# The first expert pass scatters with add into rows that hold x, instead of writing result rows that are summed later

## The reference

```python
def _L0_ffn_ref(x, Wg, W11, W12, W2):
    gate_scores = jax.nn.softmax(x @ Wg, axis=-1)          # E = 8 experts
    topk_scores, topk_idx = jax.lax.top_k(gate_scores, 2)
    topk_scores = topk_scores / (topk_scores.sum(-1, keepdims=True) + 1e-08)
    gate = jnp.einsum('bsh,ehi->bsei', x, W11)             # 256 -> 512
    value = jnp.einsum('bsh,ehi->bsei', x, W12)
    fused = gate * jax.nn.sigmoid(gate) * value
    expert_out = jnp.einsum('bsei,eih->bseh', fused, W2)   # 512 -> 256
    gathered = jnp.take_along_axis(expert_out, topk_idx[..., None], axis=2)
    return jnp.sum(topk_scores[..., None] * gathered, axis=2)

x = x + 0.5 * _L0_ffn_ref(_layernorm(x), Wg, W11, W12, W2)
x = x + _L0_attn_ref(_layernorm(x), ...)   # RMS norm, projections, short convolution, two scans, gate
x = x + 0.5 * _L0_ffn_ref(_layernorm(x), Wg, W11, W12, W2)
```

## Time and profile before

| | us |
|---|---|
| median of three runs | 966.76 |
| lowest and highest | 966.45, 969.17 |
| profiled execution, its own time | 961.58 |
| its span, first to last instruction | 959.8 |

### The profile page before, as it was taken

How to read it: one execution, slowest core, us unless ns; L and a number is a source line. 1 busy time by engine, 2 the same in 40 slices (tenths; PEclk the granted TensorE clock), 3 DMA queues, 4 the chain that set the end, 5 groups by cost and what they waited for, 6 DMA issues and landing times.

```text
span 959.8 us, 19122 instructions
## 1 busy us (share of the span) xinstructions
PE 898.3 (94%) x5429; PEld 773.5 (81%) x5430; DVE 583.2 (61%) x1386; ACT 391.8 (41%) x768; POOL 575.4 (60%) x616
## 2 busy tenths in 40 slices
PE   7869999999999999968999986999999999999994
PEld 7748888888888888846876874788888888888883
DVE  4886565665666655568745987555555555555551
ACT  3834344343443433316635775333333333333331
POOL 4836566655666665427605663577777777777762
PEclk9979999999999999979999987999999999999997
DMA  9743625526345182168202646743434433333321
GB/s 322 260 156 120 206 74 188 184 79 208 111 152 203 58 276 88 39 202 275 67 3 85 198 155 212 256 96 69 77 55 77 77 54 77 53 74 54 55 45 23
DMA packets 83745, 121.51 MB, mean 127 GB/s; under 512 B 12944, under 2 KB 62480, under 8 KB 83696
## 3 DMA queue, kind: packets, MB, share of 16 engines
q1 hardware_dynamic: 44032, 56.57, 17.9%
q0 software_dynamic: 25088, 37.59, 17.9%
q10 hardware_dynamic: 14576, 26.75, 8.2%
HBM read 73.62 MB, written 47.25 MB: 126 GB/s over the span
## 4 chain that ended last, share of the span: by engine, by line
PE 81%; DVE 7%; DMA 4%; ACT 2%; issue 2%; POOL 1%; ACTq 1%; POOLq 0%; SPq 0%; DVEq 0%
PE bank L1492 40%; PE bank L1515 21%; PE bank L1501 6%; PE bank L1614 3%; PE bank L1484 3%; PE bank L1430 3%; DMA w_lo<-w_lo_rows 2%; PE bank L1675 2%; PE bank L1631 1%; DVE states L1353 1%; DMA out_rows<-yb,idx_i 1%; PE bank L1665 1%; PE bank L1602 1%; DVE work L1361 1%; ACT work L829 1%
## 5 line engine op out<-in xcount | busy, mean ns | idle before, releaser
L1197 DVE TENSOR_TENSOR sg<-sg,bank 128x512 f32<-128x512 f32 x142 | 97.7, 688 | 281.8 <-ACT sg L758 281.8
L1492 PE MATMUL bank<-w_hi,xt_hi 128*128 x568 | 235.5, 415 | 7.0 <-DVE xt_lo L1186 6.1
L1492 PE MATMUL bank<-w_hi,xt_lo 128*128 x568 | 223.4, 393 | 0.0
L1492 PE MATMUL bank<-w_lo,xt_hi 128*128 x568 | 223.3, 393 | 0.0
L750 ACT ACTIVATE yb<-bank,gates_in 128x256 f32<-128x256 f32 x142 | 67.5, 475 | 313.3 <-PE bank L1515 273.2
L555 POOL DMA_INDIRECT xg<-xn_rows,idx_i x142 | 139.9, 986 | 62.4 <-issue 41.7
L559 POOL DMA_INDIRECT gates_in<-gate_rows,idx_g x142 | 135.6, 955 | 52.0 <-issue 42.7
L1515 PE MATMUL bank<-w_hi,ft_hi 128*128 x568 | 160.1, 282 | 2.2 <-ACT yb L750 2.2
L1515 PE MATMUL bank<-w_hi,ft_lo 128*128 x568 | 160.3, 282 | 0.0
L1515 PE MATMUL bank<-w_lo,ft_hi 128*128 x568 | 160.3, 282 | 0.0
L569 POOL DMA_INDIRECT out_rows<-yb,idx_i x71 | 114.7, 1616 | 59.9 <-ACT yb L750 45.0
(11 more groups left out here) (290 smaller groups left out, 1296.4 us busy)
## 6 DMA issues: line engine op xcount, KB each, us to landing
w_lo<-w_lo_rows SPq DMA_DIRECT2D x32, 512.0 KB, 4.5
w_lo_rows<-w_lo ACTq DMA_DIRECT2D x16, 512.0 KB
xn_rows<-work SPq DMA_DIRECT2D x14, 512.0 KB, 3.2
x_all<-x SPq DMA_DIRECT2D x8, 512.0 KB, 10.3
w_lo_rows<-in_sb ACTq DMA_DIRECT2D x16, 256.0 KB, 2.4
gate<-x SPq DMA_DIRECT2D x16, 256.0 KB, 7.3
seq<-y_rows SPq DMA_DIRECT2D x8, 512.0 KB, 5.1
seq<-w ACTq DMA_DIRECT2D x7, 512.0 KB, 4.4
```

Of the source, the lines that this page charges most:

```text
L1197: nc.vector.tensor_tensor(sg[p], sg[p], ps_g[p][:], ALU.mult).then_inc(f_step, 1)
L1492: last = nc.tensor.matmul(dst[p][:], xt[p][:, c, :], of(w), start=(c == 0 and n == 0), stop=(c == DC - 1 and n == len(parts) - 1))
```

## The change

x1_rows becomes the place of x plus the first expert part. Early in the first router ScalarE copies x to it in four DMAs of 1 MB, from memory to memory. In the first pass GpSimd scatters with add into it, with the waits that the second pass has: before add t it waits for add t-1, and ScalarE's output of tile t for add t-2. Before the first add GpSimd waits for the copies. y_rows, the loads of y_rows and of x behind the pass, the sums on VectorE and the stores of the sum go. After the last add has landed, SyncE loads the chunks of x1_rows into four places, and the statistics are taken from there.

The index of the first pass is now made as that of the second, padding in the 128 rows behind (one table operation less, two index operations more). low_up(0) of VectorE moves ahead of the indices. TensorE gets idle products between the selection steps of both routers (10 and 7, 8 and 0), and 4 ahead of the last logits of the second. In the second router variance_x2 of the last chunk moves ahead of norm_x2 of the one before, and the last normed rows are stored by ScalarE right behind its norm_x2, no more by SyncE between the loads of low parts.

```diff
-        x1_dram = nc.dram_tensor("x1_rows", [L, D], F32, kind="Internal").ap()
-        y_dram = nc.dram_tensor("y_rows", [TOPK * L + ET * P, D], F32, kind="Internal").ap()
+        x1_dram = nc.dram_tensor("x1_rows", [ROWS, D], F32, kind="Internal").ap()
...
+        x1_place = [states[:].rearrange("p a n -> p (a n)").rearrange("p (t d) -> p t d", d=D),
+                    seq[:, 0, 8 + 3 * G * D:8 + 4 * G * D].rearrange("p (t d) -> p t d", d=D), xin[0], xin[1]]
...
             sp.wait_ge(lo_out, 32 * E)
-            for i in range(NCH):
-                for h in range(2 if i < NCH // 2 else 1):
-                    load_x(i, h, x_early)
-            for p in range(2):
-                sp.wait_ge(y_out[p], 16 * ((ET + 1 - p) // 2))
-            load_y(0)
-            load_y(1)
...
-            for i in range(NCH):
-                b = i % 2
-                sp.wait_ge(summed, i + 1)
-                if 1 <= i < NCH - 2:
-                    load_y(i + 2)
-                if i < NCH - 2:
-                    sp.dma_start(rows(x1_dram, i), xin[b]).then_inc(x1_out[b], 16)
+            sp.wait_ge(added[0], 16 * ET)
+            for i in range(4):
+                load_rows(i)
+            for i in range(4, NCH):
+                sp.wait_ge(norm_ready, i - 3)
+                load_rows(i)
...
             load_low(0)
             load_low(1)
-            store_xn(NCH - 1)
...
                 def scatter(t):
                     pool.wait_ge(ye_ready, t + (base + 1))
-                    if r == 0:
-                        nc.gpsimd.indirect_dma_start(y_dram, bass.IndirectOffsetOnAxis(ap=idx_s[:, t:t + 1], axis=0), yb[t % 2], None).then_inc(y_out[t % 2], 16)
-                        return
                     if t > 0:
-                        pool.wait_ge(added, 16 * t)
-                    nc.gpsimd.indirect_dma_start(out, bass.IndirectOffsetOnAxis(ap=idx_i[:, t:t + 1], axis=0), yb[t % 2], None,
-                                                 compute_op=ALU.add).then_inc(added, 16)
+                        pool.wait_ge(added[r], 16 * t)
+                    elif r == 0:
+                        pool.wait_ge(x1_init, 16 * 4)
+                    nc.gpsimd.indirect_dma_start((x1_dram, out)[r], bass.IndirectOffsetOnAxis(ap=idx_i[:, t:t + 1], axis=0), yb[t % 2], None,
+                                                 compute_op=ALU.add).then_inc(added[r], 16)
...
                     if r == 1 and n == 2:
                         norm_x2(NCH - 1)
+                        store_last_rows()
...
-                    if r == 0 and t >= 2:
-                        act.wait_ge(y_out[t % 2], 16 * (t // 2))
-                    if r == 1 and not (isinstance(t, int) and t < 2):
-                        act.wait_ge(added, t * 16 - 16)
+                    if not (isinstance(t, int) and t < 2):
+                        act.wait_ge(added[r], t * 16 - 16)
                     nc.scalar.activation(yb[q % 2], ps_u[:, 0:D], ACT.Copy, scale=gates_in[:, q:q + 1]).then_inc(ye_ready, 1)
...
             for k in range(NCH):
                 variance_x(k)
+                if k >= NCH // 2:
+                    part_ = slice((k - NCH // 2) * 2 * CH, (k - NCH // 2 + 1) * 2 * CH)
+                    act.dma_start(x1_dram[part_, :], x[part_, :]).then_inc(x1_init, 16)
...
+                if i == NCH:
+                    variance_x2(NCH - 1)
                 if i >= 2:
                     norm_x2(i - 2)
-            variance_x2(NCH - 1)
...
                 if r == 0:
                     in_units()
+                    low_up(0)
                 indices(r)
...
-            def sum_choices(i):
-
-                first, second = y_place[y_buffer[i]]
-                dve.wait_ge(y_in[y_buffer[i]], 32 * y_buffer[0:i + 1].count(y_buffer[i]))
-                nc.vector.tensor_tensor(first, first, second, ALU.add).then_inc(half_sum, 1)
-
             def stats_x1(i, b):
...
-                nc.vector.tensor_tensor(halves(whole_), x_rows, halves(y_rows[0]), ALU.add).then_inc(summed, 1)
-                dve.wait_ge(summed, i + 1)
-                ln_stats(i + NCH, b, rows_of(b))
+                ln_stats(i + NCH, b, lambda t: x1_place[i % 4][:, t, :])
...
             def router(r):
                 for n in range(NQB):
+                    if n >= 2:
+                        idle = ((10, 7), (8, 0))[r][n - 2]
+                        keep_busy(ps_g[0][:], before.unsqueeze(1).to_broadcast([P, G, P]), idle)
...
-            pe.wait_ge(summed, 1)
+            pe.wait_ge(x1_in[0], 16)
             keep_busy(ps_t1[1][0][:], before.unsqueeze(1).to_broadcast([P, G, P]), 12)
...
                 transposes_2(i)
+            keep_busy(ps_g[0][:], before.unsqueeze(1).to_broadcast([P, G, P]), 4)
             logits_2(NCH - 1)
```

More of the change, by code:

```diff
@@ L268, in build @@
         hi11_ready, hi12_ready, lo11_ready, lo12_ready, lo_out, lo_in, xt_step = (sem(n) for n in ("hi11_ready", "hi12_ready", "lo11_ready", "lo12_ready", "lo_out", "lo_in", "xt_step"))
-        x1_out = [sem(f"x1_out{b}") for b in range(2)]
+        x1_in, x1_init = [sem(f"x1_in{b}") for b in range(4)], sem("x1_init")
         xn_x_out = [sem(f"xn_x_out{b}") for b in range(3)]
-        y_in = [sem(f"y_in{b}") for b in range(3)]
-        y_out = [sem(f"y_out{b}") for b in range(2)]
-        x_early, x_late, half_sum, summed, norm_pool, norm_act, r_ready = (sem(n) for n in ("x_early", "x_late", "half_sum", "summed", "norm_pool", "norm_act", "r_ready"))
+        norm_pool, norm_act, r_ready = (sem(n) for n in ("norm_pool", "norm_act", "r_ready"))
+        added = [sem(f"added{r}") for r in range(2)]
         x_in = [sem(f"x_in{b}") for b in range(4)]
@@ L289, in build @@
         xg_tr, xt_ready, g_done, v_done, sg_ready, f_step, f_ready = (sem(n) for n in ("xg_tr", "xt_ready", "g_done", "v_done", "sg_ready", "f_step", "f_ready"))
-        f_tr, ft_hi_ready, ft_ready, ye_done, ye_ready, added = (sem(n) for n in ("f_tr", "ft_hi_ready", "ft_ready", "ye_done", "ye_ready", "added"))
+        f_tr, ft_hi_ready, ft_ready, ye_done, ye_ready = (sem(n) for n in ("f_tr", "ft_hi_ready", "ft_ready", "ye_done", "ye_ready"))
         block = ctx.enter_context(nc.Block())
@@ L454, in _ @@
                 sp.wait_ge(xn_out[b], 16 * (NCH // 2))
-            sp.wait_ge(added, 16 * ET)
+            sp.wait_ge(added[1], 16 * ET)
         @block.gpsimd
@@ L485, in _ @@
             pool.wait_ge(const_ready, 1)
-            for dram in (xn_dram, out):
+            for dram in (xn_dram, out, x1_dram):
                 nc.gpsimd.dma_start(dram[L:ROWS, :], zeros).then_inc(pads_out, 16)
@@ L834, in take_u @@
                 act.wait_ge(u_done, c + 1)
[L835 to L836 removed]
+                if c >= NCH - 2:
+                    act.wait_ge(norm_ready, NCH - 2)
                 nc.scalar.activation(seq[:, 0, c * CH + 1:(c + 1) * CH + 1], ps_u1[b][:], ACT.Identity, scale=ssm[:, BBAR:BBAR + 1], bias=ssm[:, UBIAS:UBIAS + 1]).then_inc(u_ready, 1)
[L839 to L844 removed]
             for i in range(2):
@@ L905, in norm_x2, with store_last_rows @@
                 last.then_inc(norm_ready, 1)
+            def store_last_rows():
+                act.wait_ge(norm_ready, 2 * NCH)
+                act.dma_start(rows(xn_dram, 0), xn[(NCH - 1) % 2]).then_inc(xn_out[(NCH - 1) % 2], 16)
             act.wait_ge(fwd_done, NCH + 1)
@@ L1206, in experts @@
                 if r == 0:
-                    low_up(0)
                     low_value(0)
-                    dve.wait_ge(pads_out, 32)
+                    dve.wait_ge(pads_out, 48)
                     rows_in(0, 0)
```

72 lines of the change are left out of this document (13 added, 59 removed).

## The result

| | before | after |
|---|---|---|
| median of 4 runs each | 966.79 | 992.71 |
| lowest and highest | 966.45, 969.17 | 982.5, 995.4 |
| profiled execution, its span | 959.8 | 993.7 |

What follows compares the result with a forecast made beforehand. TensorE was taken as full in both expert passes and the mixer, so gains come only from the seams. Terms +15.3 + 8 - 3.8 - 1.4 + 0 - 1.5 = +16.6 us gave 978.2, plus 5.2 to the median 983.4; range 965 to 997.

Steps and rivals of the forecast that it cites:

- the 5.2 us between it and the median: Whole kernel: profiled execution 961.58 us against a run median of 966.76; 5.2 added to 978.2, giving 983.4.
- The lag: First pass: adds waiting for landings beside weight loads make 22.3 us of lag, 7 hidden, TensorE waits 15.3 us.
- the 2.4 us per eight tiles: First pass: the chain of adds is too long by this per eight tiles beside weights, between 1.3 and 3.9.
- the forecast's upper case: First pass: 3.9 us too long per burst, 7 x 3.9 + 7 = 34 of lag, 27 felt, +28: 995.
- the prediction's reading: First pass: by the DMA queue rule a scatter waits a few packets only, loaded steps near 4.6 us, lag nought.
- The end of the pass: End of first pass: last adds land in a row, +5.1 us without lag, 7.5 to 9 with it, taken as +8.
- The seam: Behind the first pass: one load and no sums, -3.8 us, and GpSimd's first statistics operations faster, -1.4 us.
- First router: First router: selection and index gains against +0.6 us for the copies of x (bounds 0 and +4), in sum 0.
- The third rival: First router: copies of x delay the first expert's weights by +4 us on top of the forecast: 987; chance 0.08.
- Second router: Second router: faster last logits and selection products at full clock, -1.5 us, between -2.5 and +0.5.
- The first (adds keep up, 965): First pass: adds late by less than 0.8 us, three times, leave no lag; -1.6 us, 965; chance 0.20.
- The second: Whole kernel: adds keep up and every other term takes its good end, -3.6 us, 963; chance 0.12.

Runs made afterwards that it cites:

- kernels with plain or free scatters: Changed kernel, first pass writing rows of its own: plain scatters without waiting for the previous landing (0.9957), plain with that wait (1.0012), adds without it (0.9947).
- the kernel with spread weights: Changed kernel with ScalarE issuing at most 512 KB of weight transfers behind one output: 970.44 us, ratio 1.0028 to the kernel before.

## Why the prediction was right or wrong

**The kernel before has two rhythms in its first pass.** A second trace of it was taken, on the chip of the other experiments:

> The kernel before, unchanged, for a trace from the chip of the other experiments. If the longer tile steps that the kernels with plain or free scatters show in the first pass (5.1 us, or 3.7 and 6.4 by turns, instead of 4.85) belong to the chip, this trace has them too: first pass about 343 instead of 336.7 us from first to last output. If they belong to the change (the later start of the pass shifts the engines against each other), it has 336.7 again.

Two of its outputs on ScalarE's timeline, and two lines of its windows table:

```profile
207.24 0.47 ACT L750 ACTIVATE yb<-bank,gates_in 128x256 f32<-128x256 f32 x1 [2.38 <-PE bank L1515]
212.24 0.47 ACT L750 ACTIVATE yb<-bank,gates_in 128x256 f32<-128x256 f32 x1 [2.53 <-PE bank L1515]
200.00:220.00 20.00, 20.00 (x124) 17.62 (x123) 14.55 (x27) 9.22 (x16) 11.92 (x13) 1.00 0.18 57
260.00:280.00 20.00, 18.24 (x113) 15.83 (x112) 9.09 (x18) 5.99 (x12) 10.77 (x12) 1.00 0.68 230
```

Most tiles take 5.0 to 5.1 us instead of 4.85, with shorter ones among them, and 342.0 us lie between first and last output instead of 336.7. Without weight traffic the windows still read 20.00 of 20 us busy, since the ends of products are modelled and short waits do not show. Where weights move they do not, 18.24 in 260 to 280, so a TensorE below 20.00 in such a stretch is no sign of the adds by itself; the landings that the output waits for are. The execution that I read had the short rhythm. By this one trace the 5.2 us between it and the median, which I carried over to the changed kernel as it was, are the rhythm; they lie in the very stretch that the adds slow, and the changed kernel's first tiles take 4.85. So the addition was wrong, and it hid part of the next miss. Against this second trace, whose pass takes 357.0 us, the changed kernel's is 17.4 and 15.5 us longer, near the 15.3 of the forecast, but the forecast had worked from 350.7 and 4.85. That it came within 9 us of the median is luck to this extent: without the 5.2 it is 978.2, 14.5 too low, and the first trace's span is 33.9 longer than that of the execution that was read, twice the 16.6 of the sum.

**The lag.** The mechanism was right at every point named: steps of 5.4 to 7 us and more, outputs waiting for landings, TensorE under 20.00 from the third expert on, quiet steps near 4.6. The size was not: the pass took 23.8 and 21.8 us more than the pass that I started from, not 15.3 more. The step that failed is the 2.4 us per eight tiles, between bounds of 1.3 and 3.9. In the four full bursts of the first trace three adds took 5.0, 7.2, 5.1 and 6.9 us over 4.6 each, mean 6.0; by the forecast's own sum that is 23.0 + 13.8 + 6.0 = 42.8 against 38.8, 4.0 too long: the upper bound. I left it because a late add would move its followers out of the burst. It can't: the burst is issued by the engine that waits for the adds. By 7 x 4.0 + 7 = 35 made and 7 hidden, 28 felt, the forecast's upper case, that is 4 to 6 us more than was measured, since the seven bursts are not all full ones. By the Trainium skill (DMA: Bandwidth & Descriptors, section "Queues, rings and completion order") each DMA engine goes round its queues and changes at every packet; in the prediction's reading that keeps loaded steps near 4.6. Here they were 6.8 and 7.2 beside 1 to 1.5 MB and 5.2 to 6.8 beside loads of 512 KB issued with the add, but 4.6 to 4.85 where such loads came 2.1 to 2.4 us behind it, so the traces agree with that reading in the last case and not in the others.

**The end of the pass.** Forecast +8; from the last down product to the landing 10.9 us after (443.35 to 454.25) and 3.3 before (414.29 to 417.55): +7.6. **The seam.** Forecast -5.2; from the load to the mixer 25.3 and 19.8: -5.5, of which the load took 3.9 us to the statistics, against 4.4. Both hold.

**First router.** Forecast 0, measured +5.3 and +3.1. The copies were taken at +0.6 between 0 and +4, since they had 30 us. The mechanism named (weights late for a conversion ahead of the selection) is there with 0.52 us; the larger part is one that I did not see, ScalarE's waits for the stores of normed rows to leave its buffers: 2.29 us ahead of the conversion and 2.75 one buffer earlier (2.08 and 1.93 in the second trace). The stores issued between 29 and 37 us land 10.0 to 12.7 us after their issue beside the copies, and 2.9 to 5.2 without them. The third rival was right that the copies delay the start, less in what waits for them. Besides, -0.6 of router gains was counted; with the router edits alone the trace shows 0.8 gained in the selection and 1.1 lost in the six idle products behind it.

**Second router.** Forecast -1.5, measured +0.6 and +1.0 from mixer to second pass. This stretch holds more than the router. From the last logits on (570.22 before, 602.87 after) 28.3 us passed before and 27.4 after, and 28.4 and 27.4 in the second traces: a gain of 0.9 and 1.0. The rest lies ahead of the logits, in the mixer's last output products, of before and then of after:

```profile
562.54 3.72 PE L1675 MATMUL bank<-outw_sb,work 128*128 128x256 f32 x16
593.50 5.41 PE L1622 MATMUL bank<-outw_sb,work 128*128 128x256 f32 x16
```

The granted clock reads 0.69 in 593.5 to 599, and the second trace has the same 5.40. Two of the experiments with plain or free scatters show it too (5.02 and 5.19), all other traces have 3.72; no run tells why the clock fell there. In the router itself the logits gained what I said. What was late next is the first gather. Kernel before, second trace, and then the changed one, second trace (GpSimd, SyncE's queue, TensorE):

```profile
599.59 1.09 POOL L555 DMA_INDIRECT xg<-xn_rows,idx_i  x1 [10.51 <-DMA xn_rows<-work]
602.91 0.44 PE L1484 MATMUL bank<-ident,xg 128*128 128x128 f32 x2
```

```profile
619.09 1.10 POOL L527 DMA_INDIRECT xg<-xn_rows,idx_i  x1 [10.63 <-DVE idx_i L1024]
619.20 0.80 SPq L390 DMA_DIRECT2D w_lo<-w_lo_rows  x2
624.69 0.44 PE L1431 MATMUL bank<-ident,xg 128*128 128x128 f32 x2 [1.34 <-DMA xg<-xn_rows,idx_i]
```

ScalarE's store does take the store out of the gather's wait, which now follows the indices directly. But SyncE, no longer held up by that store, issues its next megabyte 0.1 us behind the gather, and from gather to transposes it is 5.6 us instead of 3.3. I had priced the removed wait and not the queue behind it. So of this term the sign was right for the router, 0.5 us short in size, and the clock in the mixer was not in the sum at all.

**Rivals.** The first (adds keep up, 965) fails, and the kernel with spread weights shows that most of it was one edit away: 970. The second fails. Pass two was taken as unchanged and is 0.7 to 2.1 us longer; no run tells why.

## What to carry to other kernels

A chain of transfers in which each waits for the one before has a rate of its own; compare its slowest stretch, not its mean, with the engine it feeds, and look at who issues the transfers that disturb it: if that engine waits for the chain, chain and disturbance fall into step and nothing spreads by itself. Spread large transfers over the tiles first; then ask whether the work saved is on the path at all. Show the worst stretch of a change beside its best. And take two traces of the same kernel before you put a difference of a few microseconds down to a change.

## What was not expected of the hardware

Beside two loads of 512 KB, the first issued within 0.1 us of it, an add took 6.5 to 8.6 us from its start to the next one's; beside single loads of 512 KB 5.2 to 6.8 when these were issued up to 0.8 us behind its start, and 4.6 to 4.85 when 2.1 to 2.4 us behind it. One kernel's first pass ran at 4.85 or mostly 5.0 to 5.1 us a tile with the same instructions. And idle products can cost what they gain: the same six took 1.46 us behind an idle stretch of 1.56 us and 2.55 behind one of 2.31, with the granted clock at its lower level, but 1.46 again behind one of 2.60 in another kernel.
